# A post-norm decoder layer on one core: who adds beta, who scales the weights' and the queries' numbers, and when the temperature is computed

## The chip, the cores and the metric

The kernel runs on one core of one Trainium2 chip. The metric is the device time of one launch in microseconds. Before the change the median of three runs is 4235.66 us (4234.53 to 4238.19). The engines are named TensorE (PE in the profile; PEld is its weight load), VectorE (DVE), ScalarE (ACT), GpSimd (POOL) and SyncE (SP, which issues most transfers).

## The reference, cut to what matters

A layer of three parts, each followed by a residual and a layer norm: an integer-quantised self-attention, a cross-attention over a context, and a mixture-of-experts feed-forward. Only the first part is touched:

```
h = (x - mu) * rsqrt(var + eps);  h = h * fq(gamma) + fq(beta)
qkv = fq_floor(fq_floor(h) @ fq_round(w_qkv))
temp = floor(exp(log_temp) * 4096) / 4096
dots = fq_floor(einsum(q, k) * temp);  attn = fq_floor(softmax(dots))
```

x has 16 sequences of 224 rows of 512. Each `fq` divides by a power of two taken from the largest absolute value of the whole tensor, rounds to integer levels and multiplies back. So a maximum over everything must be known before the first level is computed, and stages follow one another on that account.

## The kernel before, in words

The kernel is a series of blocks (`phase(...)`). All engines meet at a block's end; at the start of the next GpSimd clears the semaphores of the one before. Within a block every engine runs its own instruction list in order and waits on semaphores.

**The first stage (block `s1`).** The 3584 rows lie in SBUF as 28 tiles of 128 rows, and `chunk(i)` is four tiles, so there are seven chunks (`NCH1`) of 2048 elements a partition. SyncE issues gamma, beta and the log of the temperature, then the seven chunks of x, then four parts (`KC`) of w_qkv (3072 elements a partition) and w_out (4096). VectorE finds the maxima of gamma and beta, takes the statistics of every tile (`bn_stats`), and from them the scales. ScalarE normalises tile after tile in place and raises `normed` once a chunk. Then VectorE runs `scaled(i)`: multiply by gamma, add beta, take the largest absolute value, each over one chunk. Between the first four chunks it takes the maximum of one part of w_qkv. GpSimd does three all-reduces over the partitions: of gamma and beta, of the weights' maxima (`w_all`), of h (`h_all`). After `w_all` VectorE computes the weights' scales and writes their int16 levels into two buffers, ScalarE casts them to bf16. Last, VectorE computes the temperature by a chain of some twenty operations on one element (lines 446 to 464), in which each waits for the one before, and then the levels of w_out, which ScalarE casts.

**The query and key stage (block `qd`).** The products of w_qkv and h are computed again in pieces, for one pair of heads at a time: a piece is one 128-row group of queries or keys by two blocks of 512 columns, the last of four by one block. `piece(m)` names it, and eight pieces make a pair of heads, of which there are eight. A piece's products are eight matmuls into two PSUM banks (four into one for the short piece). VectorE turns them into int16 levels (line 627), ScalarE casts these to bf16 into `qk` (line 645). Behind that, `dots_of(p, b)` multiplies queries by keys of one sequence and VectorE takes the largest absolute value (line 634). The pieces alternate between banks 0 to 1 and 2 to 3, the dots between banks 4 to 5 and 6 to 7. `in_order` sets one order for TensorE and VectorE alike: ahead of the dots the eight pieces of the first pair of heads; then, for each piece of the next pair, its products followed by two groups of dots of this pair.

`absolute_scale` turns a maximum into a scale by a chain of small VectorE operations and runs four times in the kernel.

Of the kernel before, what the change touches and what calls it, by code (L numbers as in the profile page):

```python
# [8 lines left out]
I32 = mybir.dt.int32  # L9
# [11 lines left out]
P = 128  # L21
# [14 lines left out]
LG = 4  # L36
# [57 lines left out]
def decoder_kernel(nc, a, out):  # L94
# [4 lines left out]
    with ctx:  # L99
# [106 lines left out]
        def absolute_scale(name, partials, unit):  # L206


            with phase("ab" + name, "red", "all", "ch") as (block, (red_done, all_done, chs)):
                @block.vector  # L210
                def _(dve):
                    V.tensor_reduce(red[:, 0:1], partials, axis=AX.X, op=ALU.max).then_inc(red_done, 1)
                    dve.wait_ge(all_done, 1)
                    ch = Chain(dve, chs)
                    ch.link(V.tensor_scalar(red[:, 1:2], red[:, 1:2], col(unit), None, ALU.mult))
                    pot_scale(nc, ch, red[:, 1:2], col("s_" + name), col("i_" + name), t8)
                    ch.link(V.tensor_scalar(col("c_" + name), col(unit), col("i_" + name), None, ALU.mult))
                    ch.link(V.reciprocal(t8[:, 0:1], col("c_" + name)))
                    ch.link(V.tensor_scalar(col("off_" + name), t8[:, 0:1], -0.5, 0.5, ALU.mult, ALU.add))

                @block.gpsimd
                def _(pool):
                    pool.wait_ge(red_done, 1)
                    G.partition_all_reduce(red[:, 1:2], red[:, 0:1], P, RMAX).then_inc(all_done, 1)
# [105 lines left out]
        with ExitStack() as st:  # L330
# [8 lines left out]
            steps = sb("scale_steps_of_two", [P, 4, 2], F32, st)  # L339
            with phase("s1", "g", "o", "r1", "r2", "r3", "a1", "a2", "a3", "var", "std", "rdy", "nrm", "wl", "wc", "ch",  # L340
                       *[f"x{i}" for i in range(NCH1)], *[f"w{k}" for k in range(KC)]) as (block, (
                    g_in, o_in, gb_red, w_red, h_red, gb_all, w_all, h_all, var_done, std_done, scale_ready, normed, w_levelled, w_cast, chs, *ins)):
                x_in, w_in = ins[:NCH1], ins[NCH1:]

                def chunk(i):
# [13 lines left out]
                @block.gpsimd  # L359
                def _(pool):  # L360
                    pool.wait_ge(gb_red, 1)
                    G.partition_all_reduce(maxima[:, 1, 0:2], maxima[:, 0, 0:2], P, RMAX).then_inc(gb_all, 1)
                    pool.wait_ge(w_red, 1)
                    G.partition_all_reduce(maxima[:, 1, 2:4], maxima[:, 0, 2:4], P, RMAX).then_inc(w_all, 1)
                    pool.wait_ge(h_red, 1)
                    G.partition_all_reduce(maxima[:, 1, 4:5], maxima[:, 0, 4:5], P, RMAX).then_inc(h_all, 1)
# [17 lines left out]
                def _(dve):  # L384
# [5 lines left out]
                    done.then_inc(gb_red, 1)  # L390

                    for i in range(NCH1):
# [25 lines left out]

                    def scaled(i):
                        dve.wait_ge(normed, i + 1)  # L420
                        x = X[:, chunk(i), :]
                        ch.link(V.tensor_tensor(x, x, gbq[:, 0, :].unsqueeze(1).broadcast_to([P, LG, D]), ALU.mult))
                        ch.link(V.tensor_tensor(x, x, gbq[:, 1, :].unsqueeze(1).broadcast_to([P, LG, D]), ALU.add))
                        ch.link(V.tensor_reduce(part[:, 8 + i:9 + i], x, axis=AX.XY, op=ALU.max, apply_absolute_value=True))
# [20 lines left out]
                    pot_scale(nc, ch, maxima[:, 1, 4:5], col("s_h"), col("i_h"), t8)  # L445

                    x, n, r, p = col("temp_log"), col("temp_n"), col("temp_r"), col("temp")
                    ni = t8[:, 0:1].bitcast(I32)
                    ch.link(V.tensor_scalar(ni, x, 1.4426950408889634, None, ALU.mult))
                    ch.link(V.tensor_copy(n, ni))  # L450
                    ch.link(V.scalar_tensor_tensor(r, n, -0.693359375, x, ALU.mult, ALU.add))
                    ch.link(V.scalar_tensor_tensor(r, n, 2.12194440e-4, r, ALU.mult, ALU.add))
                    ch.link(V.tensor_scalar(p, r, 1.0 / 5040, 1.0 / 720, ALU.mult, ALU.add))
                    for c in (1.0 / 120, 1.0 / 24, 1.0 / 6, 0.5, 1.0, 1.0):
                        ch.link(V.tensor_scalar(p, p, r, c, ALU.mult, ALU.add))

                    ch.link(V.tensor_scalar(t8[:, 1:2], n, 127.0, 8388608.0, ALU.add, ALU.mult))
                    ch.link(V.tensor_copy(t8[:, 2:3].bitcast(I32), t8[:, 1:2]))
                    ch.link(V.tensor_scalar(p, p, t8[:, 2:3], 4096.0, ALU.mult, ALU.mult))
                    ch.link(V.tensor_copy(ni, p))  # L460
                    ch.link(V.tensor_copy(t8[:, 3:4], ni))
                    ch.link(V.tensor_scalar(t8[:, 4:5], t8[:, 3:4], p, None, ALU.is_gt))
                    ch.link(V.tensor_scalar(t8[:, 3:4], t8[:, 3:4], t8[:, 4:5], 1.0 / 4096.0, ALU.subtract, ALU.mult))
                    ch.link(V.tensor_copy(p, t8[:, 3:4]))
                    dve.wait_ge(w_cast, KC - 1)
# [103 lines left out]
        with ExitStack() as st:  # L569
# [22 lines left out]
            with phase("qd", "mm", "lv", "mv", "dm", "mt", "cl") as (block, (mm_done, lv_ready, moved, d_mm, max_taken, cleared)):  # L592
                @block.tensor
                def _(pe):
# [10 lines left out]
                    def dots_of(p, b):  # L605
# [11 lines left out]
                        last.then_inc(d_mm, 1)  # L617
                    in_order(products_of, dots_of)

                @block.vector  # L620
                def _(dve):
                    def products_of(m):
                        oc, (lo, hi) = piece(m)
                        dve.wait_ge(mm_done, m + 1)
                        if m >= 2:
                            dve.wait_ge(moved, m - 1)
                        V.tensor_scalar(lv[:, m % 2, 0:hi - lo, :], psum[:, 2 * (m % 2):2 * (m % 2) + hi - lo, :], col("off_qkv"), col("c_qkv"),
                                        ALU.add, ALU.mult).then_inc(lv_ready, 1)

# [7 lines left out]
                    dve.wait_ge(cleared, 1)  # L637
                    in_order(products_of, dots_of)

                @block.scalar  # L640
                def _(act):
                    for m in range(NPAIR * UN):
                        oc, (lo, hi) = piece(m)
                        act.wait_ge(lv_ready, m + 1)
                        S.copy(qk[:, oc, lo * D:hi * D], lv[:, m % 2, 0:hi - lo, :].rearrange("p a n -> p (a n)")).then_inc(moved, 1)
            products("dots_raw", [col("s_qkv"), col("s_qkv"), col("temp")])
# [2010 lines left out]
```

## Time and profile before

| what | value |
|---|---|
| median of three runs | 4235.66 us |
| the profiled execution's own time | 4238.76 us |
| its span | 4236.8 us |
| TensorE, VectorE, ScalarE, GpSimd busy | 3414.0, 2515.7, 1629.3, 873.8 us |
| mean granted TensorE clock | 0.877 |

Busy times are sums over the whole span, and the stages have different limits, so the rows below go by stretch. The granted clock is a share of 2.4 GHz; 0.50 is 1.2 GHz. In a table by stretch the engines stand in the order PE, PEld, DVE, ACT, POOL, each with its busy time and its instructions. In the order of time, a line gives the start, the length and the engine of a run of equal instructions; what stands in brackets is idle time of that engine just before, and what ended it.

### The profile page before, as it was taken

What the parts mean: (1) busy time and instruction counts of PE and PEld (TensorE: products, weight loads), DVE (VectorE), ACT (ScalarE), POOL (GpSimd) and SP (SyncE); (2) the same over time, 40 slices, a digit from 0 to 9 for tenths busy, and PEclk for the clock granted to TensorE, in tenths of its full rate; (3) what the DMA queues carried; (4) which work ended last, traced back from release to release, by engine and by line L of the source; (5) the groups of instructions that cost most, each with busy time, mean ns of one, the idle gap of its engine ahead of it and who ended that gap; (6) DMA issues with size and microseconds to landing.
All of it is one profiled execution on the core that took longest, in us unless ns stands there. A gap on an engine that the chain in (4) does not pass through costs nothing. (4 is left out here: it accounts for less than half of the span.)

```text
span 4236.8 us, 76941 instructions
## 1 busy us (share of the span) xinstructions
PE 3414.0 (81%) x30914; PEld 2544.5 (60%) x30914; DVE 2515.7 (59%) x3831; ACT 1629.3 (38%) x3064; POOL 873.8 (21%) x710
## 2 busy tenths in 40 slices
PE   0787753269656999999999999959993399999994
PEld 0343331146325788888888888735552299999993
DVE  8669879979873555555555555537764133333333
ACT  2222269968122343343444344322221233333333
POOL 0000012200000443343443344320112311111110
PEclk9999775555687999999999999969996699999997
DMA  4500033333032000110100110031101433333325
GB/s 154 184 1 1 9 111 107 95 92 95 12 140 88 21 29 29 43 43 29 30 29 29 47 39 29 10 74 31 41 21 55 177 91 87 87 84 84 84 44 153
DMA packets 140175, 276.56 MB, mean 65 GB/s; under 512 B 43464, under 2 KB 43464, under 8 KB 135776
## 3 DMA queue, kind: packets, MB, share of 16 engines
q1 hardware_dynamic: 124208, 239.60, 18.0%
q0 software_dynamic: 14592, 30.44, 4.1%
q8 instruction: 237, 3.88, 0.4%
q10 hardware_dynamic: 1072, 2.10, 0.2%
q14 instruction: 66, 0.54, 0.0%
HBM read 158.02 MB, written 102.23 MB: 61 GB/s over the span
## 5 line engine op out<-in xcount | busy, mean ns | idle before, releaser
L1636 DVE TENSOR_REDUCE arena<-psum 112x4 f32<-112x1504 f32 x256 | 441.6, 1725 | 531.0 <-PE psum L1455 531.0
L1359 POOL TENSOR_TENSOR arena<-arena 125x896 f32<-125x896 f32 x128 | 269.8, 2108 | 830.6 <-ACT arena L1599 637.5
L1599 ACT ACTIVATE arena<-psum 125x1792 f32<-125x1792 f32 x192 | 320.3, 1668 | 160.7 <-PE psum L1469 160.7
L1367 POOL TENSOR_TENSOR arena<-arena 125x896 f32<-125x896 f32 x128 | 269.7, 2107 | 221.2 <-ACT arena L1599 216.2
L2389 POOL DMA_INDIRECT x_plus_h_rows<-arena x72 | 114.6, 1592 | 731.1 <-DVE arena L2560 726.7
L2550 DVE TENSOR_TENSOR gelu_T_rest<-arena,gelu_T_high 128x384 fp32r<-128x384 f32 (+1 forms) x192 | 104.7, 547 | 269.0 <-ACT gelu_T_high L2496 269.0
L2411 PE MATMUL psum<-tokens_T_high,w_high 128*128 128x384 f32 (+1 forms) x768 | 255.4, 333 | 1.6 <-DVE tokens_T_rest L2525 1.6
L2413 PE MATMUL psum<-tokens_T_high,w_rest 128*128 128x384 f32 (+1 forms) x768 | 254.8, 332 | 0.0
L2412 PE MATMUL psum<-tokens_T_rest,w_high 128*128 128x384 f32 (+1 forms) x768 | 254.5, 331 | 0.0
L821 ACT ACTIVATE arena<-arena,scales 112x224 bf16<-112x224 uint8 x512 | 239.7, 470 | 2.1
L760 PE MATMUL psum<-arena 64*112 64x224 bf16 x512 | 79.2, 410 | 191.3 <-DVE arena L780 178.6
L1375 PE MATMUL psum<-Wv_high,ctx_T_high 128*125 128x256 f32 x768 | 233.0, 303 | 0.0
L2411 PE MATMUL psum<-w_high,gelu_T_high 128*128 128x512 f32 (+1 forms) x576 | 228.7, 397 | 0.0
L2491 ACT ACTIVATE arena<-psum 128x384 f32<-128x384 f32 (+1 forms) x192 | 92.7, 483 | 353.4 <-PE psum L2413 352.4
L2413 PE MATMUL psum<-w_high,gelu_T_rest 128*128 128x512 f32 (+1 forms) x576 | 224.9, 390 | 0.0
L2412 PE MATMUL psum<-w_rest,gelu_T_high 128*128 128x512 f32 (+1 forms) x576 | 224.3, 389 | 0.0
L1377 PE MATMUL psum<-Wv_high,ctx_T_rest 128*125 128x256 f32 x768 | 217.0, 283 | 0.0
L1376 PE MATMUL psum<-Wv_rest,ctx_T_high 128*125 128x256 f32 x768 | 216.9, 282 | 0.0
L1375 PE MATMUL psum<-ctx_T_high,Wk_high 128*128 128x376 f32 x512 | 183.4, 358 | 0.0
L760 PEld LDWEIGHTS psum<-arena 64*112 64x112 bf16 x512 | 34.2, 187 | 236.4 <-DVE arena L780 223.2
L1376 PE MATMUL psum<-ctx_T_rest,Wk_high 128*128 128x376 f32 x512 | 171.5, 335 | 0.0
L1377 PE MATMUL psum<-ctx_T_high,Wk_rest 128*128 128x376 f32 x512 | 171.2, 334 | 0.0
(361 smaller groups left out, 8813.2 us busy)
## 6 DMA issues: line engine op xcount, KB each, us to landing
arena<-L_ffn_moe_w SPq DMA_DIRECT2D x16, 2048.0 KB, 10.8
arena<-ctx SPq DMA_DIRECT2D x16, 1500.0 KB
rows_by_slot<-arena SPq DMA_DIRECT2D x1, 18200.0 KB, 52.0
arena<-x SPq DMA_DIRECT2D x14, 1024.0 KB, 13.2
arena<-arena SPq DMA_DIRECT2D x16, 896.0 KB, 7.0
arena<-x_after_attn SPq DMA_DIRECT2D x32, 448.0 KB, 16.3
dots_ints<-arena SPq DMA_DIRECT2D x16, 784.0 KB, 4.8
arena<-dots_ints SPq DMA_DIRECT2D x16, 784.0 KB, 5.5
```

What stands on the lines that cost most here:

```text
L821: last = S.activation(junk[:, pr % 2, j, :], d8[:, u, h, (j % 2) * NS:(j % 2 + 1) * NS], ACT.Exp, scale=col("minus_s_d")[0:HALF], accum_ou ...
L1359: G.tensor_tensor(some_exps[:, r, :, :], prob[:, t, :, 0:NS], prob[:, t, :, NS:2 * NS], ALU.add).then_inc(paired, 1)
L1367: G.tensor_tensor(some_exps[:, 0, :, :], some_exps[:, 0, :, :], prob[:, 1, :, s * NS:(s + 1) * NS], ALU.add).then_inc(paired, 1)
L1375: PE.matmul(to, wh(k), xh(k), start=(k == 0), stop=False)
L1376: PE.matmul(to, wh(k), xl(k), start=False, stop=False)
L1377: last = PE.matmul(to, wl(k), xh(k), start=False, stop=(k == KC - 1))
L1599: S.activation(prob[:, t, :, :], score_psum(MC, 2 * NS), ACT.Exp, scale=SCALE2).then_inc(exp_done, 1)
L1636: return V.tensor_reduce(rmx[:, i // 2, i % 2, :], score_psum(HALF, HC), axis=AX.X, op=ALU.max).then_inc(r_free, 1)
L2389: pool.indirect_dma_start(out=base_d[:, :], out_offset=bass.IndirectOffsetOnAxis(ap=row_to[0:n, u, t:t + 1], axis=0), in_=yr[0:n, u, t, :] ...
L2411: PE.matmul(to, wh(k), xh(k), start=(k == 0), stop=False)
L2412: PE.matmul(to, wh(k), xl(k), start=False, stop=False)
L2413: last = PE.matmul(to, wl(k), xh(k), start=False, stop=(k == n - 1))
```

## The change

In the first stage the beta addition of chunks 0 to 4 (`BY_POOL` is 5) moves to GpSimd, which does it in place as soon as VectorE has multiplied a chunk. VectorE does gamma and beta of chunks 5 and 6, and takes the maxima later in its list, by `largest(i)`. GpSimd's all-reduce of the weights' maxima stands behind its fifth addition. The temperature's chain is moved unchanged from the end of VectorE's list to the place between the maxima of gamma and beta and the first statistics. In the query and key stage ScalarE writes the levels from PSUM (scale `c_qkv`, bias `low_qkv`, a new constant of `absolute_scale`), and VectorE casts them; VectorE's list has a unit's two maxima ahead of the cast, TensorE's list is as before.

```diff
+                ch.link(V.tensor_scalar(col("low_" + name), col("c_" + name), 0.5, -0.5, ALU.mult, ALU.add))
...
-                    pool.wait_ge(w_red, 1)
-                    G.partition_all_reduce(maxima[:, 1, 2:4], maxima[:, 0, 2:4], P, RMAX).then_inc(w_all, 1)
+                    for i in range(NCH1):
+                        if i < BY_POOL:
+                            pool.wait_ge(multiplied, i + 1)
+                            G.tensor_tensor(X[:, chunk(i), :], X[:, chunk(i), :], gbq[:, 1, :].unsqueeze(1).broadcast_to([P, LG, D]), ALU.add).then_inc(shifted, 1)
+                        if i == KC:
+                            pool.wait_ge(w_red, 1)
+                            G.partition_all_reduce(maxima[:, 1, 2:4], maxima[:, 0, 2:4], P, RMAX).then_inc(w_all, 1)
...
+                    (the temperature's chain, ahead of the statistics)
...
-                    def scaled(i):
+                    def gamma(i):
                         dve.wait_ge(normed, i + 1)
                         x = X[:, chunk(i), :]
-                        ch.link(V.tensor_tensor(x, x, gbq[:, 0, :]..., ALU.mult))
-                        ch.link(V.tensor_tensor(x, x, gbq[:, 1, :]..., ALU.add))
-                        ch.link(V.tensor_reduce(part[:, 8 + i:9 + i], x, ...))
+                        V.tensor_tensor(x, x, gbq[:, 0, :]..., ALU.mult).then_inc(multiplied, 1)
+                        if i >= BY_POOL:
+                            dve.wait_ge(multiplied, i + 1)
+                            V.tensor_tensor(x, x, gbq[:, 1, :]..., ALU.add).then_inc(shifted, 1)
+                    def largest(i):
+                        dve.wait_ge(shifted, i + 1)
+                        ch.link(V.tensor_reduce(part[:, 8 + i:9 + i], X[:, chunk(i), :], ...))
                     for i in range(KC):
-                        scaled(i)
+                        gamma(i)
                         dve.wait_ge(w_in[i], 16)
                         ch.link(V.tensor_reduce(part[:, i:i + 1], qkvw[:, i, :], ...))
+                        if i >= 1:
+                            largest(i - 1)
...
-                    scaled(KC)
+                    gamma(KC)
+                    largest(KC - 1)
+                    gamma(KC + 1)
                     dve.wait_ge(w_all, 1)
...
-                    for i in range(KC + 1, NCH1):
-                        scaled(i)
+                    gamma(KC + 2)
+                    for i in range(KC, NCH1):
+                        largest(i)
...
-            def in_order(products_of, dots_of):
+            def in_order(products_of, dots_of, products_first):
...
-                        if p + 1 < NPAIR:
+                        if p + 1 < NPAIR and products_first:
                             products_of((p + 1) * UN + i)
                         for b in range(i * NB // UN, (i + 1) * NB // UN):
                             dots_of(p, b)
+                        if p + 1 < NPAIR and not products_first:
+                            products_of((p + 1) * UN + i)
...
-                        V.tensor_scalar(lv[...], psum[...], col("off_qkv"), col("c_qkv"), ALU.add, ALU.mult).then_inc(lv_ready, 1)
+                        dve.wait_ge(lv_ready, m + 1)
+                        V.tensor_copy(qk[:, oc, lo * D:hi * D], lv[...]).then_inc(moved, 1)
...
-                        act.wait_ge(lv_ready, m + 1)
-                        S.copy(qk[:, oc, lo * D:hi * D], lv[...]).then_inc(moved, 1)
+                        act.wait_ge(mm_done, m + 1)
+                        if m >= 2:
+                            act.wait_ge(moved, m - 1)
+                        S.activation(lv[...], psum[...], ACT.Identity, bias=col("low_qkv"), scale=col("c_qkv")).then_inc(lv_ready, 1)
```

## Rows read from the trace of the kernel before

**Rows 1.** Busy time by stretch: stretch, length, engines (instructions), clock, DMA share, GB/s.
```profile
0.00:126.00 126.00, 0.00 (x0) 0.00 (x0) 106.12 (x143) 35.97 (x35) 6.91 (x10) 1.00 0.34 129
307.60:494.50 186.90, 146.70 (x833) 57.74 (x832) 174.62 (x168) 52.62 (x56) 0.00 (x0) 0.89 0.00 1
```
**Rows 2.** Order of time in the first stage, VectorE, GpSimd, ScalarE.
```profile
11.74 2.47 DVE L395 BATCH_NORM_STATS2 arena<-arena 128x6 f32<-128x512 f32 x4 [2.57 <-DMA arena<-x]
...
41.38 2.29 DVE L423 TENSOR_TENSOR arena<-arena 128x2048 f32<-128x2048 f32 x1
43.70 2.29 DVE L424 TENSOR_REDUCE part_max<-arena 128x1 f32<-128x2048 f32 x1
46.02 3.35 DVE L429 TENSOR_REDUCE part_max<-arena 128x1 f32<-128x3072 f32 x1
...
85.20 2.31 POOL L364 PARTITION_ALL_REDUCE arena<-arena  x1 [75.45 <-DVE arena L432]
...
115.54 0.15 DVE L449 TENSOR_SCALAR scale_steps<-scales 128x1 int32<-128x1 f32 x1
...
119.67 2.35 DVE L466 TENSOR_SCALAR arena<-arena,scales 128x4096 int16<-128x4096 f32 x1
122.06 3.61 ACT L381 CAST arena<-arena 128x4096 bf16<-128x4096 int16 x1 [4.15 <-DVE arena L466]
```

**Rows 3.** Order of time in the cross-attention, GpSimd and then VectorE.
```profile
1381.10 2.10 POOL L1367 TENSOR_TENSOR arena<-arena 125x896 f32<-125x896 f32 x1
1383.16 2.08 POOL L1359 TENSOR_TENSOR arena<-arena 125x896 f32<-125x896 f32 x1
...
1382.89 0.34 DVE L1641 TENSOR_TENSOR arena<-arena 112x8 f32<-112x8 f32 x1
1383.26 2.02 DVE L1642 TENSOR_SCALAR arena<-arena 112x8 bf16<-112x8 f32 x1
```

**Rows 4.** One line, an all-reduce: durations in ns (min/median/max), first and last start.
```profile
L204 POOLq MODIFY_POOL_CONFIG  x2: 11/11/11, 860.9 to 860.9; - x2
L204 POOL PARTITION_ALL_REDUCE red_max<-red_max x1: 379/379/379, 866.5 to 866.5; - x1
```

**Rows 5.** Order of time in the query and key stage, TensorE and VectorE.
```profile
330.40 1.90 PE L601 MATMUL psum<-arena 128*128 128x512 bf16 x8
330.63 2.09 DVE L634 TENSOR_REDUCE arena<-psum 112x1 f32<-112x896 f32 x2
...
332.23 0.40 PE L615 MATMUL psum<-arena 64*112 64x224 bf16 x4
332.63 1.35 DVE L627 TENSOR_SCALAR arena<-psum,scales 128x1024 int16<-128x1024 f32 x1
...
332.78 0.40 PE L615 MATMUL psum<-arena 64*112 64x224 bf16 x4 [0.15 <-DVE arena L634]
333.11 1.90 PE L601 MATMUL psum<-arena 128*128 128x512 bf16 x8
333.88 2.10 DVE L634 TENSOR_REDUCE arena<-psum 112x1 f32<-112x896 f32 x2
...
356.74 3.17 PE L601 MATMUL psum<-arena 128*128 128x512 bf16 x8
```

**Rows 6.** Busy time by stretch in that stage, columns as in the first group.
```profile
342.52:356.19 13.67, 10.89 (x61) 4.27 (x62) 12.56 (x13) 3.76 (x4) 0.00 (x0) 0.87 0.00 0
349.55:352.80 3.25, 2.63 (x16) 1.06 (x16) 3.25 (x5) 1.05 (x1) 0.00 (x0) 1.00 0.00 0
352.80:356.04 3.24, 1.77 (x12) 0.67 (x12) 3.24 (x4) 1.05 (x1) 0.00 (x0) 0.99 0.00 0
```

**Rows 7.** Groups of instructions (count, busy us, mean ns), the last by its line.
```profile
L1017 DVE CAST arena<-arena 128x4096 bf16<-128x4096 int16 x7 | 8.6, 1227 | 0.2
...
L1599 ACT ACTIVATE arena<-psum 125x1792 f32<-125x1792 f32 x192 | 320.3, 1668 | 160.7 <-PE psum L1469 160.7
...
L219 DVE TENSOR_SCALAR scales<-scale_steps x4: 153/154/154, 289.3 to 1183.4; 128x1 f32<-128x1 f32 x4
```

More of the change, by code:

```diff
@@ L339, in decoder_kernel @@
             steps = sb("scale_steps_of_two", [P, 4, 2], F32, st)
-            with phase("s1", "g", "o", "r1", "r2", "r3", "a1", "a2", "a3", "var", "std", "rdy", "nrm", "wl", "wc", "ch",
+            with phase("s1", "g", "o", "r1", "r2", "r3", "a1", "a2", "a3", "var", "std", "rdy", "nrm", "gx", "bx", "wl", "wc", "ch",
                        *[f"x{i}" for i in range(NCH1)], *[f"w{k}" for k in range(KC)]) as (block, (
-                    g_in, o_in, gb_red, w_red, h_red, gb_all, w_all, h_all, var_done, std_done, scale_ready, normed, w_levelled, w_cast, chs, *ins)):
+                    g_in, o_in, gb_red, w_red, h_red, gb_all, w_all, h_all, var_done, std_done, scale_ready, normed, multiplied, shifted, w_levelled, w_cast, chs, *ins)):
                 x_in, w_in = ins[:NCH1], ins[NCH1:]
+                BY_POOL = NCH1 - 2
                 def chunk(i):
@@ L390, in _ @@
                     done.then_inc(gb_red, 1)
+                    x, n, r, p = col("temp_log"), col("temp_n"), col("temp_r"), col("temp")
+                    ni = t8[:, 0:1].bitcast(I32)
+                    ch.link(V.tensor_scalar(ni, x, 1.4426950408889634, None, ALU.mult))
+                    ch.link(V.tensor_copy(n, ni))
+                    ch.link(V.scalar_tensor_tensor(r, n, -0.693359375, x, ALU.mult, ALU.add))
+                    ch.link(V.scalar_tensor_tensor(r, n, 2.12194440e-4, r, ALU.mult, ALU.add))
+                    ch.link(V.tensor_scalar(p, r, 1.0 / 5040, 1.0 / 720, ALU.mult, ALU.add))
+                    for c in (1.0 / 120, 1.0 / 24, 1.0 / 6, 0.5, 1.0, 1.0):
+                        ch.link(V.tensor_scalar(p, p, r, c, ALU.mult, ALU.add))
+                    ch.link(V.tensor_scalar(t8[:, 1:2], n, 127.0, 8388608.0, ALU.add, ALU.mult))
+                    ch.link(V.tensor_copy(t8[:, 2:3].bitcast(I32), t8[:, 1:2]))
+                    ch.link(V.tensor_scalar(p, p, t8[:, 2:3], 4096.0, ALU.mult, ALU.mult))
+                    ch.link(V.tensor_copy(ni, p))
+                    ch.link(V.tensor_copy(t8[:, 3:4], ni))
+                    ch.link(V.tensor_scalar(t8[:, 4:5], t8[:, 3:4], p, None, ALU.is_gt))
+                    ch.link(V.tensor_scalar(t8[:, 3:4], t8[:, 3:4], t8[:, 4:5], 1.0 / 4096.0, ALU.subtract, ALU.mult))
+                    ch.link(V.tensor_copy(p, t8[:, 3:4]))
                     for i in range(NCH1):
@@ L417, in _ @@
                     V.scalar_tensor_tensor(stat[:, :, 5], stat[:, :, 6], -1.0, stat[:, :, 2], ALU.mult, ALU.mult).then_inc(scale_ready, 1)
-                    def scaled(i):
+                    def gamma(i):
                         dve.wait_ge(normed, i + 1)
                         x = X[:, chunk(i), :]
-                        ch.link(V.tensor_tensor(x, x, gbq[:, 0, :].unsqueeze(1).broadcast_to([P, LG, D]), ALU.mult))
-                        ch.link(V.tensor_tensor(x, x, gbq[:, 1, :].unsqueeze(1).broadcast_to([P, LG, D]), ALU.add))
-                        ch.link(V.tensor_reduce(part[:, 8 + i:9 + i], x, axis=AX.XY, op=ALU.max, apply_absolute_value=True))
+                        V.tensor_tensor(x, x, gbq[:, 0, :].unsqueeze(1).broadcast_to([P, LG, D]), ALU.mult).then_inc(multiplied, 1)
+                        if i >= BY_POOL:
+                            dve.wait_ge(multiplied, i + 1)
+                            V.tensor_tensor(x, x, gbq[:, 1, :].unsqueeze(1).broadcast_to([P, LG, D]), ALU.add).then_inc(shifted, 1)
+                    def largest(i):
+                        dve.wait_ge(shifted, i + 1)
+                        ch.link(V.tensor_reduce(part[:, 8 + i:9 + i], X[:, chunk(i), :], axis=AX.XY, op=ALU.max, apply_absolute_value=True))
                     for i in range(KC):
-                        scaled(i)
+                        gamma(i)
                         dve.wait_ge(w_in[i], 16)
                         ch.link(V.tensor_reduce(part[:, i:i + 1], qkvw[:, i, :], axis=AX.X, op=ALU.max, apply_absolute_value=True))
+                        if i >= 1:
+                            largest(i - 1)
                     dve.wait_ge(o_in, 16)
@@ L445, in _ @@
                     pot_scale(nc, ch, maxima[:, 1, 4:5], col("s_h"), col("i_h"), t8)
[L447 to L464, printed above, removed]
                     dve.wait_ge(w_cast, KC - 1)
@@ L617, in dots_of @@
                         last.then_inc(d_mm, 1)
-                    in_order(products_of, dots_of)
+                    in_order(products_of, dots_of, True)
                 @block.vector
@@ L623, in products_of @@
                         oc, (lo, hi) = piece(m)
[L624 to L628, printed above, removed]
+                        dve.wait_ge(lv_ready, m + 1)
+                        V.tensor_copy(qk[:, oc, lo * D:hi * D], lv[:, m % 2, 0:hi - lo, :].rearrange("p a n -> p (a n)")).then_inc(moved, 1)
                     def dots_of(p, b):
@@ L637, in _ @@
                     dve.wait_ge(cleared, 1)
-                    in_order(products_of, dots_of)
+                    in_order(products_of, dots_of, False)
                 @block.scalar
@@ L643, in _ @@
                         oc, (lo, hi) = piece(m)
-                        act.wait_ge(lv_ready, m + 1)
-                        S.copy(qk[:, oc, lo * D:hi * D], lv[:, m % 2, 0:hi - lo, :].rearrange("p a n -> p (a n)")).then_inc(moved, 1)
+                        act.wait_ge(mm_done, m + 1)
+                        if m >= 2:
+                            act.wait_ge(moved, m - 1)
+                        S.activation(lv[:, m % 2, 0:hi - lo, :], psum[:, 2 * (m % 2):2 * (m % 2) + hi - lo, :], ACT.Identity,
+                                     bias=col("low_qkv"), scale=col("c_qkv")).then_inc(lv_ready, 1)
             products("dots_raw", [col("s_qkv"), col("s_qkv"), col("temp")])
```

## The prediction

> **What bounds the kernel now.** I read the page first, to see that no single engine fills the span, so that a change is worth what its own stage says; then the busy time by stretch. The change touches two stretches, both led by VectorE [rows 1]: in 0 to 126 us it is busy 106.12 us and TensorE not at all, and in 307.60 to 494.50 us it is busy 174.62 of 186.90 us, beside 146.70 us of TensorE and 52.62 us of ScalarE. Stages are separated by barriers, so what either stretch gives up moves all that follows. I then read the order of time in both. In the first, VectorE does gamma, beta, maximum and weight maximum without a gap, and the end is set by the last weight cast on ScalarE, 122.06 + 3.61 = 125.67 us [rows 2]. In the second, two maxima of 2.00 us together and one levelling make a unit, back to back on VectorE [rows 5]; four units (three of two blocks of 512 columns, one of a single block) take 13.67 us [rows 6].
>
> **The change, first stage.** Five of seven beta additions leave VectorE. One costs 43.70 - 41.38 = 2.32 us there [rows 2], so 5 x 2.32 = 11.6 us go. The temperature's chain, 119.67 - 115.54 = 4.1 us [rows 2], leaves the end, where nothing covers it. In front VectorE idles 2.57 us before the first rows land; the statistics then run without a gap, so 4.1 - 2.6 = 1.5 us come back.
>
> What GpSimd now does is not in the trace in this size. Its additions of 896 elements take 2.10 us [rows 3]; 2048 elements lie between that (no growth) and 2048/896 times it, 4.8 us. I take 4.7, the upper end less a little for what is fixed in each. Five additions are 23.5 us; VectorE needs about 8 us a chunk (2.3 gamma, 3.4 weight maximum, 2.3 maximum [rows 2]), so GpSimd keeps up, and each chunk's maximum is taken one chunk late. The cover fails twice, for a reason that the trace shows: a VectorE addition of 8 elements with two inputs in SBUF took 0.34 us and ended with GpSimd's addition (1381.10 + 2.10), and the 112x8 operation behind it took 2.02 us and ended with the next one (1383.16 + 2.08) [rows 3]. GpSimd waits likewise: an all-reduce of 0.38 us [rows 4] took 2.31 beside a VectorE multiplication [rows 2]. So chunk 1's gamma, ready 3.4 us after GpSimd took chunk 0, waits 4.7 - 3.4 = 1.3 us. Chunk 5's gamma, ready 2.3 us after GpSimd took chunk 4, waits 2.4 us.
>
> The Trainium skill, "SBUF — State Buffer", section "Who interferes with whom", speaks against this edit: the port pair that VectorE and GpSimd share is held for a whole instruction and the later one stands still. Were VectorE never held, chunk 1's 1.3 us would be saved and the stage would gain 10.3 us in place of the 9.0 below (chunk 5's wait would turn into a wait for the all-reduce).
>
> A second cost is in the order of GpSimd's work. An all-reduce behind ordinary operations is preceded by a MODIFY_POOL_CONFIG; it started 866.5 - 860.9 = 5.6 us after it, and VectorE stood waiting [rows 4]. The weights' all-reduce now stands behind the fifth addition, which makes one switch to the additions (long before the first is wanted, so hidden) and one back. Bounds: if the switch runs beside the addition, nothing is late; if it begins at its end, the result is there 5.6 + 0.4 us later. Meanwhile VectorE does chunk 5's gamma and beta, 4.6 us, so it waits 6.0 - 4.6 = 1.4 us. I take the second. Queued behind that wait are the weights' levels and all that ScalarE casts. The sum: 11.6 + 4.1 - 1.5 - 1.3 - 2.4 - 1.4 = 9.1, less 0.1 for semaphores: 9.0 us gained, ends 4 (every addition and the switch once more late) and 12.
>
> **The change, query and key stage.** The levelling of 1024 columns out of PSUM leaves VectorE for ScalarE, and ScalarE's cast comes to VectorE, behind the unit's maxima. VectorE's cast from int16 to bf16 is in the trace: 4096 elements in 1227 ns [rows 7]. A VectorE instruction of one element in 1.1 ns (2048 in 2.29 [rows 2]) would need 4.6 us for that, so it is the fast form: 0.26 ns an element and 0.16 fixed. 1024 then take 0.43 us, 512 0.29; back to back 0.09 less each, as the levelling shows (1.35 long, followed 1.25 later [rows 5]). Lower end 0.2, upper end 1.25 us (no gain). I take 0.34 and 0.20. Four units are 4 x 2.00 + 3 x 0.34 + 0.20 = 9.22 us on VectorE.
>
> Now TensorE's order counts. Products take 1.83 us (330.40 to the next dots at 332.23), a group of dots 0.40, and products follow a group's start by 0.33 [rows 5]. A group needs the maximum two groups before it, because there are two pairs of banks. The loop: the second maximum of unit i-1 ends 2.08 us after its unit began; 0.05 to the dots, 0.33 to the products, 1.83 for them, 0.40 for the next dots, 0.05 back: 4.74 us for two units, against 4.68 for VectorE alone. Three of the four steps are of two blocks, so two units take at least 4.74 twice: 9.5 us for four units. TensorE's own work is below that (3 x 2.49 + 1.6 = 9.1). 186.90 us are 14 such groups of four: 14 x 9.5 = 133.0, so 53.9 us go.
>
> ScalarE's levelling lies under 1.67 us (1792 elements out of PSUM [rows 7]); about 1.1 by scale. It starts when the products end, and VectorE reaches the cast only after the next dots and two maxima, 0.40 + 2.08 = 2.5 us later, so it is hidden; were it the full 1.67 us and the cover gone, it would cost that much a unit. Its wait for the cast two units earlier has nothing but its own next levelling behind it. In the eight products ahead of the first dots, levelling and cast follow one another as before (1.1 + 0.4 for 1.35 + 1.05): 1 us gained. The scale's extra operation runs four times, at 0.15 us [rows 7], 0.2 with its link: 0.8 us lost.
>
> Sum against the profiled execution: 9.0 + 53.9 + 1.0 - 0.8 = 63.1 us of 4238.76, thus 4175.7. That execution is 3.1 us above the median of the runs, so I forecast **4173 us**.
>
> **Rivals.** *The clock falls in every group of four.* Now the products at 356.74 take 3.17 us in place of 1.90 [rows 5]: the clock is at 1.2 instead of 2.4 GHz, after a single-block unit in which TensorE was busy 1.77 of 3.24 us (0.55); it stayed up through units at 2.63 of 3.25 (0.81) [rows 6]. After the change the single-block unit is 1.77 of about 2.35 (0.75), nearer the second row, hence my forecast. If it falls all the same, 3.17 - 1.90 = 1.3 us and little slack: 14 x 1.3 = 18 us, 4191.
>
> *The change does not take effect on VectorE:* the cast runs at one element a cycle, 1.25 us, as the levelling did. Then the second stage stays at 186.9 and only 9 us go: 4226. The row of 1227 ns speaks against it.
>
> *The first stage gives nothing:* the adds hold VectorE each time and the switch is late by twice 5.6 us. 9 us lost from the forecast: 4182. The order (a weight maximum of 3.4 us between two gammas) speaks against it.
>
> *Slower: TensorE at 1.2 GHz through the whole of the second stage.* Eight matmuls then take 3.4 us, two groups of dots 0.9: 3 x 4.3 + 2.6 = 15.5 us for four units, longer than now. 14 x 15.5 = 217, 30 us more, less the 9: 4257. It decides from 14.0 us per four units, where the loss eats the first stage's 9. For it: the clock does fall in this stage, 0.87 over four units, and TensorE would be the bound. Against: the same rows have 1.00 where TensorE is busiest [rows 6].
>
> **How the numbers follow.** Forecast 0.65, clock falls 0.20, first stage empty 0.08, slow cast 0.04, slower 0.03. Down: VectorE alone at 9.22 (4 us) and 12 us in the first stage (3) give 4166. Up: the clock's 18 us and some of the first stage give 4196. Below 0.2% (8.5 us) a measurement can't tell from no change. Faster 0.94 (the slow cast lies at its edge, and I count half), same 0.03, slower 0.03.
>
> **What would show it.** Right: five additions of 4.7 us on GpSimd, gammas of chunk 1 and 5 of 3.6 and 4.7 us in place of 2.29, an idle of 1 to 2 us on VectorE before the weights' scale, the last weight cast ending near 117 us; casts of 0.43 us on VectorE and 9.5 us per four units, with the granted clock near 1.00. Wrong: casts above 1 us, matmuls of 8 in 3 us within the stage, or VectorE idle between maxima for more than 0.3 us.

## The result and the profile after

The changed kernel takes 4179.95 us (median of 4 runs, 4177.32 to 4183.96), beside 4236.92 us of the kernel before: ratio 0.9867, 95% interval 0.985 to 0.9884. The forecast was 4173 us, so the gain is 57 us where 63 were forecast. In two of the series further down one execution each, of 5355.62 and 5323.18 us at a granted clock of 0.633, lies far above the others and is left out of the medians and ratios given there. The profiled execution took 4178.14 us (span 4176.2, granted clock 0.880), 60.6 us less than that of before; the step by step account below is made between these two.

| place | before | after | gained up to here |
|---|---|---|---|
| last weight cast ends (first stage) | 125.67 | 115.64 | 10.0 |
| first products of the query and key stage | 289.98 | 280.31 | 9.7 |
| its first dots | 307.61 | 297.65 | 10.0 |
| its dots of the last pair of heads (no products beside them) | 494.55 | 433.17 | 61.4 |
| span | 4236.8 | 4176.2 | 60.6 |

The stretches of the kernel after (length, then PE, PEld, DVE, ACT, POOL busy, clock, DMA share, GB/s), beside [rows 1]:

```profile
0.00:116.00 116.00, 0.00 (x0) 0.00 (x0) 97.42 (x138) 35.89 (x35) 27.53 (x15) 1.00 0.37 140
297.65:433.17 135.52, 122.82 (x833) 53.16 (x832) 131.16 (x168) 61.47 (x56) 0.00 (x0) 1.00 0.00 1
```

In the second stretch the same 833 matmul records take 122.82 us in place of 146.70, and the granted clock is 1.00 throughout, where it was 0.89. VectorE is still the busiest engine, with 131.16 of 135.52 us.

The order of time in the first stage after:

```profile
13.28 2.47 DVE L421 BATCH_NORM_STATS2 arena<-arena 128x6 f32<-128x512 f32 x4
...
40.56 2.29 DVE L448 TENSOR_TENSOR arena<-arena 128x2048 f32<-128x2048 f32 x1 [2.99 <-ACT arena L383]
42.77 3.35 DVE L460 TENSOR_REDUCE part_max<-arena 128x1 f32<-128x3072 f32 x1
42.95 4.53 POOL L369 TENSOR_TENSOR arena<-arena 128x2048 f32<-128x2048 f32 x1 [32.49 <-DVE arena L448]
46.15 3.47 DVE L448 TENSOR_TENSOR arena<-arena 128x2048 f32<-128x2048 f32 x1
...
75.58 2.28 DVE L448 TENSOR_TENSOR arena<-arena 128x2048 f32<-128x2048 f32 x1
77.95 4.50 POOL L369 TENSOR_TENSOR arena<-arena 128x2048 f32<-128x2048 f32 x1 [7.92 <-DVE arena L448]
80.10 4.50 DVE L448 TENSOR_TENSOR arena<-arena 128x2048 f32<-128x2048 f32 x1
84.63 2.29 DVE L451 TENSOR_TENSOR arena<-arena 128x2048 f32<-128x2048 f32 x1
88.15 0.37 POOL L372 PARTITION_ALL_REDUCE arena<-arena  x1 [5.71 <-issue]
88.56 0.17 DVE L321 TENSOR_SCALAR arena<-arena 128x2 f32<-128x2 f32 x1 [1.64 <-POOL arena L372]
...
112.04 3.60 ACT L389 CAST arena<-arena 128x4096 bf16<-128x4096 int16 x1
```

Two multiplications by gamma (L448) are long, 3.47 and 4.50 us in place of 2.29, and both end 2.1 us behind the end of the GpSimd addition that began before them (42.95 + 4.53 = 47.48 and 46.15 + 3.47 = 49.62; 77.95 + 4.50 = 82.45 and 80.10 + 4.50 = 84.60): the multiplication stands until the addition is through and then takes about its own time. GpSimd's all-reduce starts 5.71 us after the last addition, and VectorE stands 1.64 us for it.

The order of time in the query and key stage after, over the seam between two pairs of heads, beside [rows 5, 6]. L620 are the products, L663 ScalarE's levels, L644 VectorE's cast, L634 the dots, L650 the maxima:

```profile
336.82 2.09 DVE L650 TENSOR_REDUCE arena<-psum 112x1 f32<-112x896 f32 x2 [0.50 <-PE psum L634]
...
343.71 0.40 PE L634 MATMUL psum<-arena 64*112 64x224 bf16 x4 [0.60 <-DVE arena L650]
...
346.31 2.09 DVE L650 TENSOR_REDUCE arena<-psum 112x1 f32<-112x896 f32 x2
346.39 1.90 PE L620 MATMUL psum<-arena 128*128 128x512 bf16 x8
348.22 0.63 PE L634 MATMUL psum<-arena 64*112 64x224 bf16 x8
348.32 0.42 DVE L644 CAST arena<-arena 128x1024 bf16<-128x1024 int16 x1
348.33 1.21 ACT L663 ACTIVATE arena<-psum,scales 128x1024 int16<-128x1024 f32 x1 [1.15 <-PE psum L620]
348.66 2.09 DVE L650 TENSOR_REDUCE arena<-psum 112x1 f32<-112x896 f32 x2
...
355.39 0.29 DVE L644 CAST arena<-arena 128x512 bf16<-128x512 int16 x1
355.47 1.20 ACT L663 ACTIVATE arena<-psum,scales 128x1024 int16<-128x1024 f32 x1 [2.48 <-PE psum L620]
355.73 0.59 PE L634 MATMUL psum<-arena 64*112 64x224 bf16 x8 [0.30 <-DVE arena L644]
356.18 1.09 DVE L650 TENSOR_REDUCE arena<-psum 112x1 f32<-112x896 f32 x1 [0.50 <-PE psum L634]
...
433.17 0.59 PE L634 MATMUL psum<-arena 64*112 64x224 bf16 x8 [2.13 <-DVE arena L644]
433.61 16.06 DVE L650 TENSOR_REDUCE arena<-psum 112x1 f32<-112x896 f32 x16 [0.50 <-PE psum L634]
```

Within a pair, maxima and casts follow one another on VectorE with hardly a gap (9.22 us of work by the prediction's sum in 9.49), and eight matmuls take 1.90 us behind the short unit too. A group of four units takes 9.49 us (336.82 to 346.31). At the seam the next pair's first dots wait for the short piece's cast, which now stands behind that unit's maxima, and VectorE waits 0.50 us for the dots: this group takes 9.87 us (346.31 to 356.18), and a pair 19.36.

### The profile page after: what moved, and what is told of

Same layout as the page of the kernel before. It is cut to its first block and busy times, and to the rows that moved or that the text cites. A ratio compares the mean times of both kernels' runs of the same rounds, so it can differ in the third digit from the quotient of the medians.

```text
span 4176.2 us, 76952 instructions
## 1 busy us (share of the span) xinstructions
PE 3389.6 (81%) x30914; PEld 2539.0 (61%) x30914; DVE 2457.1 (59%) x3830; ACT 1636.0 (39%) x3064; POOL 893.2 (21%) x715
## 6 DMA issues: line engine op xcount, KB each, us to landing
arena<-x SPq DMA_DIRECT2D x14, 1024.0 KB, 13.2
```

## The experiments

Line numbers shift by a few from kernel to kernel; the shapes tell which operation a row is. Diffs go against the changed kernel, or against the kernel before where the sentence says so.

**The two parts apart.** First the first stage alone (the kernel before with the first stage of the change):

```diff
+            BY_POOL = NCH1 - 2
...
+                            G.tensor_tensor(X[:, chunk(i), :], X[:, chunk(i), :], ..., ALU.add).then_inc(shifted, 1)
```

> First stage as changed, query and key stage as before. Theory (the stages are apart, VectorE leads both): the last weight cast ends near 115.6 us as in the changed kernel, 10.0 us earlier than before, and the whole run is 9 to 11 us shorter than before, about 4226. Rival (the first stage's gain is given back behind it, or belongs to both edits together): the cast ends earlier, but the whole run is within 4 us of before.

Measured: 4229.44 us (4224.95 to 4232.1, 10 runs), before 4237.67, ratio 0.998 (0.997 to 0.999). The next block starts at 115.81 us in place of 125.98, and the query and key stage keeps the clock's fall behind each short unit; the eight matmuls there take over 3 us, 13.7 us apart:

```profile
347.54 3.26 PE L617 MATMUL psum<-arena 128*128 128x512 bf16 x8
...
361.28 3.21 PE L617 MATMUL psum<-arena 128*128 128x512 bf16 x8
```

Then the query and key stage alone (the kernel before with that stage of the change):

```diff
...
-                        V.tensor_scalar(lv[...], psum[...], col("off_qkv"), col("c_qkv"), ALU.add, ALU.mult).then_inc(lv_ready, 1)
+                        V.tensor_copy(qk[:, oc, lo * D:hi * D], lv[...]).then_inc(moved, 1)
...
```

> Query and key stage as changed, first stage as before. Theory: 61 us from the first dots to the dots without products turn into 135.5 us for seven pairs of heads, 51 us gained, less 0.8 for the four extra scale operations, so about 4186. The last levels of the weights end at 125.7 us as before. Rival (the clock stayed up because the first stage had changed what came before): matmuls of eight in 3.2 us come back in the stage and it gives 33 us or less, 4203 or more.

Measured: 4188.94 us (4187.94 to 4193.42, 4 runs), before 4237.67, ratio 0.9888 (0.9871 to 0.9904). The stretch of its dots with products beside them (186.90 us before; the 61 us of the expectation is the gain of both parts up to its end):

```profile
307.60:443.00 135.40, 121.50 (x818) 53.16 (x832) 130.73 (x167) 61.42 (x56) 0.00 (x0) 1.00 0.00 1
```

The parts are worth 8.2 and 48.7 us; together 56.9, and both at once gave 57.0. As far as the scatter shows, they add.

**The temperature's chain alone in front** (against the kernel before; the chain's lines moved, nothing else):

```diff
                     done.then_inc(gb_red, 1)
+                    x, n, r, p = col("temp_log"), ...   (the chain)
```

> Kernel before with the temperature's chain alone put in front. Theory: 4.1 us go at the end of the first stage, 1.5 come back ahead of the statistics (start 13.3 instead of 11.7 us), so the last weight cast ends 2.6 us earlier, at 123.1 us. Rival (the rows land later when VectorE is late, or ScalarE's casts end the stage anyway): 0 to 1 us, cast end above 124.5.

Measured: 4230.78 us in one run. The statistics start at 13.20 us and the last weight cast ends at 122.97, 2.7 us sooner than in [rows 2]:

```profile
119.37 3.60 ACT L381 CAST arena<-arena 128x4096 bf16<-128x4096 int16 x1
```

So of the first stage's 10.0 us the chain gives 2.7; the other 7.3 come of the additions moved to GpSimd and the order that goes with them.

**The order on VectorE.** The change does two things at once in the query and key stage: it swaps the two engines' tasks, and it puts VectorE's task behind the maxima. First the swap without the order:

```diff
-                    in_order(products_of, dots_of, False)
+                    in_order(products_of, dots_of, True)
```

> Changed kernel with VectorE's cast ahead of a unit's two maxima instead of behind them. Theory (the order matters: the cast then waits for products and levelling of its own unit, a loop of 2.08 + 0.05 + 0.33 + 1.9 + 1.25 + 0.34 = about 5.95 us for two units in place of 4.74): four units take about 11.5 to 11.9 us instead of 9.5, the stage is 28 to 34 us longer, the run about 4208 to 4214. Rival (only the shorter work of VectorE counts, its order does not): within 4 us of the changed kernel, about 4180.

Measured: 4228.35 us (4213.02 to 4238.8, 10 runs), ratio to the kernel before 0.9971 (0.9956 to 0.9986). The profiled execution is the slowest of the ten:

```profile
352.69 1.21 ACT L663 ACTIVATE arena<-psum,scales 128x1024 int16<-128x1024 f32 x1 [5.36 <-PE psum L620]
...
353.93 0.43 DVE L644 CAST arena<-arena 128x1024 bf16<-128x1024 int16 x1 [3.00 <-ACT arena L663]
...
359.91 0.43 DVE L644 CAST arena<-arena 128x1024 bf16<-128x1024 int16 x1 [1.21 <-ACT arena L663]
...
362.73 3.53 PE L620 MATMUL psum<-arena 128*128 128x512 bf16 x8
```

VectorE stands for the levels in every second unit, 1.21 us at full clock and 3.00 us behind the short unit, where the clock has fallen and eight matmuls take 3.53 us. The group is 13.61 us: the expectation was too low, because it had left the clock out. Then the order without the swap (the kernel before, with VectorE's levelling behind the maxima):

```diff
...
-                    in_order(products_of, dots_of)
+                    in_order(products_of, dots_of, False)
```

> Kernel before; in the query and key stage VectorE still levels out of PSUM and ScalarE still casts, but VectorE's levelling stands behind a unit's two maxima. With the experiment that moved the cast ahead this fills the table of two by two: who does what, and in which order. Theory A (shorter work of VectorE is the gain, its order only lets it through): VectorE stays the bound at 3.25 us a unit, four units take 12.5 us if the clock holds and 13.7 if it falls as before, so 0 to 17 us gained, 4220 to 4237. Theory B (the order is the gain): four units near 10 us, 50 us gained, about 4186.

Measured: 4241.46 us (median of nine runs, 4236.45 to 4245.0), before 4238.18, ratio 1.0009 (0.9999 to 1.0019), so theory B is out. VectorE's work is the same 3.25 us a unit as before, and the clock still falls (L603 are the products):

```profile
357.91 3.46 PE L603 MATMUL psum<-arena 128*128 128x512 bf16 x8 [0.85 <-DVE arena L629]
```

In the stage, then: the order alone gives nothing. The swap alone gives nothing clear of the scatter: 4228.35 beside 4229.44 with the old stage, with 26 us between its fastest and its slowest run; from the first dots to the last maximum the profiled executions take 503.30 - 299.77 = 203.5 and 502.33 - 298.28 = 204.1 us. Both together give 49.5 (4229.44 to 4179.95). Neither half can be priced by itself.

**What the fallen clock costs.** Four matmuls whose results are unused fill TensorE's idle in the short unit, first in the kernel before:

```diff
                         last.then_inc(mm_done, 1)
+                        if hi - lo == 1:
+                            for _ in range(4):
+                                PE.matmul(psum[:, 2 * (m % 2) + 1, :], qkvw_q[:, 0, 0:P], hT[:, 0, 0:D], start=True, stop=True)
```

> The kernel before, with four more matmuls of 512 columns behind the products of each short piece, into the PSUM bank that this piece leaves unused; what they compute is not used. They lie in TensorE's idle of 0.88 us before the next dots, so by themselves they take nothing. Theory (the granted clock falls behind the short unit because TensorE is idle in it, and VectorE then waits 1.11 us for products at 1.2 GHz): the clock stays at 1.00, the group of four units takes 13.67 - 1.11 = 12.56 us, 14 groups give 15.5 us, about 4221 us. Rival (the clock falls on the whole stage's load, or the more work the more it falls): groups stay at 13.67 us or longer, 4237 us or more.

Measured: 4227.28 us (4218.86 to 4236.36, 11 runs), before 4237.79, ratio 0.9972 (0.9963 to 0.9981). L606 are the added matmuls, and the eight matmuls behind the short unit's dots take 1.90 us, where before took 3.17 [rows 5]:

```profile
340.40 1.04 PE L601 MATMUL psum<-arena 128*128 128x512 bf16 x4
341.18 2.08 DVE L637 TENSOR_REDUCE arena<-psum 112x1 f32<-112x896 f32 x2
341.28 1.03 PE L606 MATMUL psum<-arena 128*128 128x512 bf16 x4
...
343.65 1.90 PE L601 MATMUL psum<-arena 128*128 128x512 bf16 x8
...
480.94 18.05 DVE L637 TENSOR_REDUCE arena<-psum 112x1 f32<-112x896 f32 x18
```

The groups take 12.46 us in place of 13.67 (dots at 343.32 and 355.78). More work made the stage shorter and kept the clock at 1.00, so here the fall goes with the idle, not with the load. The last row of maxima starts at 480.94 us in place of 493.31, though the first began 0.8 us later: 13.2 us, not 15.5, for in the kernel before the fall shows in 11 groups, not in 14. The profiled execution, the slowest of the eleven, gave most of this back later: 9.6 us ahead at the first exponentials of the cross-attention, it is 2.8 ahead behind it, and the code there is the same. The profiled execution with the cast ahead, also the slowest of its series, did likewise: 8.1 us ahead at the last maximum (503.30 against 511.37), it ends level with that of before. Why, no run here shows. The same four matmuls in the kernel with the cast ahead:

> The changed kernel with VectorE's cast ahead of the two maxima, and the same four unused matmuls behind each short piece. Theory (the order costs through the loop products, ScalarE's levels, VectorE's cast, maximum, dots: 5.99 us for two units; the rest of that kernel's 13.61 us is the fallen clock): groups of 2 x 5.99 = 11.98 us at clock 1.00, 14 x (13.61 - 11.98) = 22.8 us less than that kernel's profiled 4238.8 us, about 4216 us; still 2.5 us a group (35 us) behind the changed kernel. Rival (the order's loss is all of the clock's making): groups of 9.5 us, about 4181 us. Rival (the clock has nothing to do with TensorE's idle): groups of 13.6 us, about 4238 us.

Measured: 4214.61 us (4207.03 to 4215.77, 5 runs), ratio to the kernel before 0.9946 (0.9933 to 0.996). The groups take 11.98 us (casts at 343.33 and 355.31), and the loop is seen at full clock:

```profile
343.33 0.43 DVE L647 CAST arena<-arena 128x1024 bf16<-128x1024 int16 x1 [1.21 <-ACT arena L666]
...
343.67 2.08 DVE L653 TENSOR_REDUCE arena<-psum 112x1 f32<-112x896 f32 x2
...
345.81 0.40 PE L637 MATMUL psum<-arena 64*112 64x224 bf16 x4 [0.60 <-DVE arena L653]
...
346.14 1.90 PE L620 MATMUL psum<-arena 128*128 128x512 bf16 x8
...
348.08 1.21 ACT L666 ACTIVATE arena<-psum,scales 128x1024 int16<-128x1024 f32 x1 [3.72 <-PE psum L620]
...
349.32 0.43 DVE L647 CAST arena<-arena 128x1024 bf16<-128x1024 int16 x1 [1.37 <-ACT arena L666]
```

Cast 0.34, two maxima 2.08, dots 0.33 and products 1.94 up to ScalarE's start, its levels 1.21, and 0.09 between them: 5.99 us for two units. By the medians the order is worth 48 us (4228.35 to 4179.95). Of these 35 are this loop (4214.61 to 4179.95; 14 x (11.98 - 9.49) = 35), and 14 the clock, which the four matmuls keep up (4228.35 to 4214.61).

**Is VectorE or TensorE the bound after the change?** The cast done twice (the first copy unused):

```diff
...
+                        V.tensor_copy(unused[:, m % 2, 0:(hi - lo) * D], lv[...])
                         V.tensor_copy(qk[:, oc, lo * D:hi * D], lv[...]).then_inc(moved, 1)
```

> Changed kernel with every cast of the query and key stage done twice, the first into an unused buffer: VectorE has 0.34 us more a unit. Theory (the loop over TensorE's order, 4.74 us for two units, and VectorE's sum of 4.68 lie so close that more work on VectorE decides at once): four units 4 x 2.00 + 3 x 0.68 + 0.40 = 10.4 us instead of 9.5, 13 us more over 14. Rival (TensorE alone is the bound now, VectorE has room): under 4 us more.

Measured: 4190.78 us in one run, 12.6 above the profiled execution of the changed kernel; a group takes 10.40 us (L635 are the dots):

```profile
346.63 0.90 PE L635 MATMUL psum<-arena 64*112 64x224 bf16 x8
...
357.03 0.90 PE L635 MATMUL psum<-arena 64*112 64x224 bf16 x8
```

The added casts, 3 x 0.33 + 0.20 = 1.19 us a group, cost 0.91: the loop over TensorE had left VectorE 0.3 us of slack. So in the changed kernel that loop sets the pace, and VectorE's own sum lies 0.3 us a group below it.

**The two terms that the profile after showed as waits.** Four additions on GpSimd, its all-reduce behind the fourth:

```diff
-            BY_POOL = NCH1 - 2
+            BY_POOL = NCH1 - 3
...
-                        if i == KC:
+                        if i == KC - 1:
                             pool.wait_ge(w_red, 1)
...
-                            V.tensor_tensor(x, x, ..., ALU.add).then_inc(shifted, 1)
+                            ch.link(V.tensor_tensor(x, x, ..., ALU.add))
...
```

> Changed kernel with four additions on GpSimd instead of five and the weights' all-reduce behind the fourth; VectorE adds beta to three chunks. Theory (chunk 5's gamma was held 2.2 us by the fifth addition, and VectorE idled 1.6 us for the switch back to the all-reduce): one addition of 2.3 us more on VectorE, 2.2 and 1.6 less, so the last weight cast ends 1.5 us earlier, at 114.1 us; chunk 4's and 5's gammas take 2.29 us, no idle ahead of the weights' scale. Rival (the idle was for something other than the switch): the idle stays, and the cast ends at 115.6 us or later.

Measured: 4175.57 us in one run; the last weight cast ends at 114.40 us, 1.24 sooner where 1.5 were expected, and chunk 5's multiplication takes 2.29 us again:

```profile
82.54 2.29 DVE L448 TENSOR_TENSOR arena<-arena 128x2048 f32<-128x2048 f32 x1
...
110.80 3.60 ACT L389 CAST arena<-arena 128x4096 bf16<-128x4096 int16 x1
```

VectorE goes on to the weights' scale without standing, at 87.19 us. And the short piece's cast ahead of its maxima:

```diff
-                        if p + 1 < NPAIR and products_first:
+                        if p + 1 < NPAIR and (products_first or i == UN - 1):
...
-                        if p + 1 < NPAIR and not products_first:
+                        if p + 1 < NPAIR and not (products_first or i == UN - 1):
```

> Changed kernel, but the cast of a pair's last (short) piece stands ahead of its unit's two maxima. Theory (the first dots of the next pair wait for that cast: 0.3 us on TensorE at each of six pairs, 2.1 us at the last): the waits on the cast go, pairs take 19.0 us instead of 19.35, the dots without products start 3 to 4 us earlier; run 4176 to 4177. Rival (the levelling of the short piece isn't done by then, VectorE waits for it): no gain or a loss up to 5 us.

Measured: 4178.82 us (4177.93 to 4185.52, 4 runs), ratio to the kernel before 0.9863 (0.9845 to 0.9881). A pair of heads takes 19.13 us in place of 19.36, and the wait ahead of the last pair is gone: 2.0 us in the stage where 3 to 4 were expected. Of the 2.1 us that TensorE stood at the last pair, VectorE had stood only 0.50, and 0.15 us of each pair's 0.38 stay: behind a pair's first cast the maxima start 0.53 us after it (320.38 to 320.91), in the changed kernel 0.35 (338.82 to 339.17). Both together, in two series:

> The changed kernel with four additions on GpSimd (the all-reduce of the weights' maxima behind the fourth) and with the short piece's cast ahead of its two maxima. If the two savings add: 1.2 us from the first stage and about 2 us from the query and key stage (2.1 at the last pair of heads, 0.2 at each of the seven pairs, less what the first part's maxima wait), so 4177 us against 4180 of the changed kernel, ratio to the kernel before 0.986. If the savings are within the noise of a run: 4180 us, 0.987.

> The kernel of the run before this one (four additions on GpSimd, the short piece's cast ahead of its maxima), for the place of its savings. If the two savings add: the last weight cast ends near 114.4 us, the seven pairs of heads take 19.13 us each in place of 19.35, the last pair's first dots don't wait, and the whole takes 4174 to 4177 us, 3 to 6 us less than the changed kernel. If they don't add, one of these three marks is missing and the time is 4180 us.

Measured: 4175.7 us in the first series (median of four runs, 4175.2 to 4181.28), ratio 0.9858 (0.9843 to 0.9873), and 4176.21 us in the second (4172.0 to 4180.35, 4 runs), 0.9859 (0.9843 to 0.9876). In the second's profile:

```profile
75.67 2.28 POOL L372 PARTITION_ALL_REDUCE arena<-arena  x1 [5.79 <-DVE arena L466]
...
110.66 3.60 ACT L389 CAST arena<-arena 128x4096 bf16<-128x4096 int16 x1
...
427.70 0.62 DVE L645 CAST arena<-arena 128x1024 bf16<-128x1024 int16 x2
...
428.24 18.04 DVE L651 TENSOR_REDUCE arena<-psum 112x1 f32<-112x896 f32 x18
```

All three marks are there: the cast ends at 114.26, pairs take 19.13 us, and eighteen maxima run through without a gap into the last pair. The maxima end at 428.24 + 18.04 = 446.28 us, against 433.61 + 16.06 = 449.67 in the changed kernel: 3.4 us. Of the versions timed more than once it has the lowest ratio, but its interval and the changed kernel's overlap, and the two were not timed side by side.

## Why the prediction was right, and where it was 2.5 us off

**First stage: 9.0 forecast, 10.0 measured.** GpSimd's addition takes 4.50 to 4.53 us where 4.7 was taken by scale. The Trainium skill, "GPSIMD Engine Reference", section "Elementwise — side-by-side cycle accounting", gives 4497 ns for an addition of this size, and the trace agrees. Chunk 1's multiplication was held 1.2 us (1.3 forecast), chunk 5's 2.2 (2.4), the wait for the all-reduce is 1.64 (1.4), the front costs 13.28 - 11.74 = 1.5 (1.5). With these the sum is 9.2. Of the other 0.8, 0.7 lies in a thing not priced: most operations that the change takes apart are no longer chained to the next by a semaphore, so that the next starts 2.21 us later in place of 2.32 (the weight maximum behind the multiplication at 40.56 starts at 42.77; where a beta addition still waits for its multiplication, at 93.22 and 95.55, it is 2.33); there are six such places. VectorE's two long multiplications had their price in the sum. The Trainium skill, "SBUF — State Buffer", section "Who interferes with whom", has the rule for them: whichever of VectorE and GpSimd starts first holds the port pair that they share for its whole instruction, and the other stands. The trace agrees in both places, with 3.47 and 4.50 us.

**Query and key stage: 53.9 forecast, 51.4 measured.** This is the mis-sized term. The casts cost what was taken (419 and 287 ns, the forecast 430 and 290), ScalarE's levels take 1.20 us where 1.1 was taken and are covered as forecast, and a group of four takes 9.49 us where 9.5 was forecast. But 14 x 9.5 took the fourteen groups as alike. Seven of them end at the seam of two pairs, where the dots wait for the whole next pair's casts, and the last of these now stands behind two maxima: 7 x (19.36 - 2 x 9.49) = 2.7 us, 135.5 us in place of 133.0. The prediction followed the cast's wait on VectorE and ScalarE, and not the wait that `dots_of` has on it for its first group. One of its own signs of being wrong shows there: VectorE stands 0.50 us between maxima at each seam. With that cast put forward this wait is gone and a pair takes 0.23 us less.

**The small terms.** The head gained 0.3 us (first products to first dots) where 1.0 was forecast: TensorE waits there only for the levels to leave PSUM, not for the cast behind them, twice for 0.58 us before (at 298.98 and 305.78) and twice for 0.43 after (at 289.17 and 295.82). Around the stage 0.36 us were lost ahead of its first products and 0.78 behind the last pair's first dots, 1.1 in all, where 0.8 was forecast for the four extra scale operations. The one ahead of the stage shows as 0.19 us (from L219 to the first products 280.31 - 279.45 = 0.86 us in place of 289.98 - 289.31 = 0.67); what the other three and the rest cost singly is not shown here. The sum of the profiled executions is 10.03 - 0.36 + 0.29 + 51.42 - 0.78 = 60.6 us against 63.1.

**The rest of the difference.** 60.6 us between the profiled executions are 57.0 between the medians: the profiled execution of before lay 1.8 us above the median of the runs beside it, and that of after 1.8 below its own. The forecast had taken 3.1 us off for the first of these. So of the 7 us between 4173 and 4179.95, 2.5 are the sum's, and the other 4.5 lie within the scatter of single executions.

**The rivals.** The clock did not fall after the change: 1.00 over the whole stretch. The runs with four unused matmuls show that the prediction looked at the right place (TensorE's idle in the short unit) and that the fall cost 1.2 us in each of 11 groups before, so some 13 of the 51 us come from the clock that stays up. After the change TensorE stands idle once in the short unit, 0.60 us (at 343.71), where it stood 0.88 and 0.60 before. But the prediction's ground, how busy TensorE is in that unit, does not settle it alone: the eight matmuls at 330.40 [rows 5] follow a unit with the same 1.77 us of 3.24 and ran at full clock. The forecast that the clock stays up held; why it stays is shown only as far as the idle goes. The slow cast and the empty first stage are refuted by the rows of casts and additions; TensorE at 1.2 GHz through the stage by the clock.

## What to carry to other kernels

When an engine is relieved of work in a loop, write out the loop through the other engines before and after, with the order on each: here the same swap of tasks gives nothing clear of the scatter with the cast ahead of the maxima and 50 us with the cast behind them. Price the seams apart from the steady groups, above all where one instruction waits for a whole batch of another's results. And where the granted clock falls in each turn of a loop, its cost is a wait like any other; here it went when the idle ahead of it was filled.

## What the runs showed of the hardware

In the kernel before, adding 64 matmuls shortened the stage by 13 us. Behind the short piece's products TensorE stands idle for 0.88 us, and in 11 of the 13 places where eight matmuls follow that piece's unit the granted clock then drops to 0.50 of full (1.2 GHz), so that they take 3.17 us in place of 1.90. Filling the idle with 1.03 us of work kept the clock at 1.00. The first two of the 13 places have the same idle and kept the clock without the filling, so the idle doesn't decide alone; what the others differ in, no run here shows. The rows are of the kernel before, the first two in the order of time, the others by stretch:

```profile
329.07 0.40 PE L615 MATMUL psum<-arena 64*112 64x224 bf16 x4 [0.88 <-DVE arena L634]
...
355.19 0.40 PE L615 MATMUL psum<-arena 64*112 64x224 bf16 x4 [0.88 <-DVE arena L634]
...
326.67:329.91 3.24, 1.77 (x12) 0.66 (x12) 3.24 (x4) 1.05 (x1) 0.00 (x0) 1.00 0.00 0
356.74:359.20 2.46, 2.46 (x8) 0.89 (x7) 2.11 (x3) 0.62 (x1) 0.00 (x0) 0.50 0.02 7
```

GpSimd's change from additions to an all-reduce cost 5.71 us in the changed kernel, released by nothing that the profile shows, as in [rows 4] with 5.6. With the all-reduce one addition earlier the gap is 5.79 us too, but VectorE's maximum for it also came only then, so that run adds no second price.
